# One attention stage of a fused tower: which of VectorE and GpSimd forms the products and the weighted values

## The reference

```python
x = jnp.roll(x, -W // 2, axis=1)                      # W = 64
qkv = (xw @ w_qkv.T).reshape(B * nw, W, 3, H, C // H)  # H = 8, C = 128
attn = jnp.einsum('bwhd,bwgd->bwhg', q, k) * SCALE     # 8 x 8 scores for each token
attn = jax.nn.softmax(attn, axis=-1)
out = jnp.einsum('bwhg,bwgd->bwhd', attn, v)
out = out.transpose(0, 2, 1, 3).reshape(B * nw, W, C)
out = out @ w_proj.T + b_proj                          # then rolled back, added to x
```

## Time and profile before

| | us |
|---|---|
| median of three timed runs | 1608.4 (1603.88, 1608.4, 1612.2) |
| the profiled execution | 1606.17 |
| its span, first to last instruction | 1604.5 |
| the stage in it, first matmul of q, k and v to the end of the last add | 103.3 |

### The profile page before, as it was taken

How to read it: one execution, slowest core, us unless ns; L and a number is a source line. 1 busy time by engine, 2 the same in 40 slices (tenths; PEclk the granted TensorE clock), 3 DMA queues, 4 the chain that set the end, 5 groups by cost and what they waited for, 6 DMA issues and landing times. The chain is left out here.

```text
span 1604.5 us, 29750 instructions
## 1 busy us (share of the span) xinstructions
PE 1141.8 (71%) x10322; PEld 781.8 (49%) x10330; DVE 1158.3 (72%) x2211; ACT 729.9 (45%) x1093; POOL 727.9 (45%) x626
## 2 busy tenths in 40 slices
PE   5857999984489445968777777777777785646770
PEld 3725565663389425744444444444444444435550
DVE  5666556455435447348999999999999995658983
ACT  4233443431045221025777777777767763011540
POOL 2213333231386657123555565555556553215655
PEclk9889999997589777769999999999999986858995
DMA  4052000001168300000000000000000000013772
GB/s 125 1 163 85 2 2 2 2 3 53 40 193 227 98 4 0 0 1 1 1 1 0 0 0 0 0 0 0 0 0 0 0 0 1 2 28 89 211 211 71
DMA packets 83243, 64.92 MB, mean 40 GB/s; under 512 B 13931, under 2 KB 73606, under 8 KB 82886
## 3 DMA queue, kind: packets, MB, share of 16 engines
q1 hardware_dynamic: 62726, 46.80, 10.5%
q0 software_dynamic: 4096, 8.40, 1.8%
q10 hardware_dynamic: 16320, 8.40, 1.8%
HBM read 43.64 MB, written 22.28 MB: 41 GB/s over the span
## 5 line engine op out<-in xcount | busy, mean ns | idle before, releaser
L2118 POOL TENSOR_TENSOR ta_ex<-ta_ex,ta_left 128x1024 f32<-128x1024 f32 x128 | 302.0, 2359 | 279.5 <-ACT ta_left L2061 279.5
L1962 PE MATMUL ta_ps_s<-ta_kT,ta_qz 128*128 (+1 forms) x512 | 258.6, 629 | 36.7 <-ACT ta_ex L2045 35.6
L1993 PE MATMUL ta_ps_t<-consts,ta_ex 128*128 128x128 f32 x1024 | 142.3, 283 | 111.7 <-POOL ta_ex L2118 53.0
L1993 PEld LDWEIGHTS ta_ps_t<-consts,ta_ex 128*128 128x128 f32 x1024 | 113.5, 144 | 176.0 <-POOL ta_ex L2118 137.6
L2149 DVE MAX8 ta_top<-ta_ps_s 128x8 f32<-128x1024 f32 x128 | 156.3, 1221 | 34.3 <-PE ta_ps_s L1962 33.7
L2045 ACT ACTIVATE ta_ex<-ta_ps_s,ta_ntop 128x1024 f32<-128x1024 f32 x128 | 142.7, 1115 | 49.1 <-DVE ta_left L2155 36.7
L2155 DVE MATCH_REPLACE8 ta_left<-ta_top,ta_ps_s 128x1024 f32<-128x1024 f32 x128 | 155.3, 1213 | 0.0
L2160 DVE MAX8 ta_top<-ta_left 128x8 f32<-128x1024 f32 x128 | 154.6, 1208 | 0.0
L2165 DVE MATCH_REPLACE8 ta_left<-ta_top,ta_left 128x1024 f32<-128x1024 f32 x128 | 154.6, 1208 | 0.0
L1962 PEld LDWEIGHTS ta_ps_s<-ta_kT,ta_qz 128*128 128x128 f32 x512 | 89.5, 195 | 119.1 <-issue 104.8
L2061 ACT ACTIVATE ta_left<-ta_left,ta_ntop 128x1024 f32<-128x1024 f32 x128 | 146.3, 1143 | 0.8
(11 more groups left out here) (623 smaller groups left out, 2532.4 us busy)
## 6 DMA issues: line engine op xcount, KB each, us to landing
l1e_w<-in_L_ffn_W_dram SPq DMA_DIRECT2D x46, 256.0 KB
l3e_packed<-l3f_packed SPq DMA_DIRECT2D x64, 160.0 KB, 2.9
l3f_rows<-l1f_zero SPq DMA_DIRECT2D x2, 2048.0 KB, 13.0
l3e_x<-l3f_rows SPq DMA_DIRECT2D x32, 128.0 KB, 2.9
l3e_outs<-l3e_y ACTq DMA_DIRECT2D x32, 128.0 KB, 2.7
l1f_rows<-l1f_zero SPq DMA_DIRECT2D x2, 1472.0 KB, 9.4
l1e_x<-l1f_rows SPq DMA_DIRECT2D x46, 64.0 KB
l1e_outs<-l1e_y ACTq DMA_DIRECT2D x46, 64.0 KB
```

The lines of the kernel that those rows point to most:

```text
L1962: ins = pe.matmul(ps_s[:, i % 2, half * BANK:(half + 1) * BANK], qz[:, odd, h, :], kT[:, grp, bass.ds(at.key0[i // PAIR] + half * BANK, BA ...
L1993: ins = pe.transpose(ps_t[:, j * P:(j + 1) * P], ex[:, i % 4, j * P:(j + 1) * P], m.ident)
L2118: pool.tensor_tensor(ex[:, i % 4, :], ex[:, i % 4, :], left[:, i % 4, :], ALU.subtract).then_inc(kept, 1)
```

## The change

VectorE forms the weighted values of all four tiles of a group. It also forms all four products of group 0, and those of tiles 2 and 3 of the later groups; GpSimd forms those of tiles 0 and 1 of groups 1 to 3 and nothing else. GpSimd begins group 1 when VectorE's products of group 0 are done, and group g from 2 on when the weighted values of group g - 2 are done. VectorE's list is now, for each g: scores of g (tiles 2, 3, 0, 1), products of tiles 2 and 3 of g + 1, weights of g, weighted values of g; `add(0)` stays behind the weighted values of group 2, and the scores of group 3, which were ahead of it, are behind it. The matmul and copy of q, k and v go tile by tile: 16 copies of 384 columns, each with its own signal, in place of 4 of 1536. TensorE's turning waits for VectorE alone, tile by tile. The core of the diff:

```diff
+        def operands(g, t):
+            q = qkv[:, g, t, 0:D].rearrange("p (h d) -> p h d", h=H).unsqueeze(2).broadcast_to([P, H, H, HW])
+            k = qkv[:, g, t, D:2 * D].rearrange("p (h d) -> p h d", h=H).unsqueeze(1).broadcast_to([P, H, H, HW])
+            return qk[:, slot(g, t), :, :, :], q, k
...
                 for t in range(4):
                     n = 4 * g + t
-                    ins = pe.matmul(ps_q[:, t, 0:3 * D], ...)
-                ins.then_inc(qkv_ready, 1)
+                    if g >= 1:
+                        pe.wait_ge(qkv_in, n - 3)
+                    pe.matmul(ps_q[:, t, 0:3 * D], ...).then_inc(qkv_ready, 1)
...
-                    if t < 3:
-                        pe.wait_ge(av_dve, 3 * g + t + 1)
-                    else:
-                        pe.wait_ge(av_pool, g + 1)
+                    pe.wait_ge(av_ready, 4 * g + t + 1)
...
-            for g in range(GROUPS):
-                act.wait_ge(qkv_ready, g + 1)
-                act.activation(qkv[:, g, :, :], ps_q[:, :, 0:3 * D], ACT.Copy).then_inc(qkv_in, 1)
+            for n in range(TILES):
+                act.wait_ge(qkv_ready, n + 1)
+                act.activation(qkv[:, n // 4, n % 4, :], ps_q[:, n % 4, 0:3 * D], ACT.Copy).then_inc(qkv_in, 1)
...
-            products(0)
-            for g in range(GROUPS):
-                if g + 1 < GROUPS:
-                    products(g + 1)
-                pool.wait_ge(weighed, g + 1)
-                if g >= 2:
-                    pool.wait_ge(o_turned, g - 1)
-                out, a, v = factors(g, 3)
-                pool.tensor_tensor(out, a, v, ALU.mult).then_inc(av_pool, 1)
+            for g in range(1, GROUPS):
+                pool.wait_ge(qkv_in, 4 * g + 4)
+                if g == 1:
+                    pool.wait_ge(qk_ready, 4)
+                else:
+                    pool.wait_ge(av_ready, 4 * (g - 1))
+                for t in range(2):
+                    out, q, k = operands(g, t)
+                    pool.tensor_tensor(out, q, k, ALU.mult).then_inc(qk_pool, 1)
...
+            def products(g, tiles):
+                for t in tiles:
+                    dve.wait_ge(qkv_in, 4 * g + t + 1)
+                    out, q, k = operands(g, t)
+                    dve.tensor_tensor(out, q, k, ALU.mult).then_inc(qk_ready, 1)
...
-            scores(0)
+            products(0, range(4))
             for g in range(GROUPS):
+                scores(g)
                 if g + 1 < GROUPS:
-                    scores(g + 1)
+                    products(g + 1, (2, 3))
                 weights(g)
                 dve.wait_ge(weighed, g + 1)
                 if g >= 2:
                     dve.wait_ge(o_turned, g - 1)
-                for t in range(3):
+                for t in range(4):
                     out, a, v = factors(g, t)
-                    dve.tensor_tensor(out, a, v, ALU.mult).then_inc(av_dve, 1)
+                    dve.tensor_tensor(out, a, v, ALU.mult).then_inc(av_ready, 1)
                 if g == 2:
                     add(0)
             add(B - 1)
```

More of the change, by code:

```diff
@@ L1595, in stage_l2_attn @@
             sem(x) for x in ("max_done", "shifted", "exps", "sum_done", "inverted", "weighed"))
-        av_dve, av_pool, o_turned, oT_in, spread, y_in, regrouped, yT_in, out_ready, out_used = (
-            sem(x) for x in ("av_dve", "av_pool", "o_turned", "oT_in", "spread", "y_in", "regrouped", "yT_in", "out_ready", "out_used"))
+        av_ready, qk_pool, o_turned, oT_in, spread, y_in, regrouped, yT_in, out_ready, out_used = (
+            sem(x) for x in ("av_ready", "qk_pool", "o_turned", "oT_in", "spread", "y_in", "regrouped", "yT_in", "out_ready", "out_used"))
         block = ctx.enter_context(nc.Block())
@@ L1615, in _ @@
             for g in range(GROUPS):
-                if g >= 1:
-                    pe.wait_ge(qkv_in, g)
                 for t in range(4):
                     n = 4 * g + t
-                    ins = pe.matmul(ps_q[:, t, 0:3 * D], m.xnT[:, n * P:(n + 1) * P], m.wqkv2[:, :, :].rearrange("p c d -> p (c d)"),
-                                    start=True, stop=True)
-                ins.then_inc(qkv_ready, 1)
+                    if g >= 1:
+                        pe.wait_ge(qkv_in, n - 3)
+                    pe.matmul(ps_q[:, t, 0:3 * D], m.xnT[:, n * P:(n + 1) * P], m.wqkv2[:, :, :].rearrange("p c d -> p (c d)"),
+                              start=True, stop=True).then_inc(qkv_ready, 1)
             pe.wait_ge(bias_in, 16)
@@ L1663, in exponentials @@
                 if g >= 2:
[L1664 to L1665 removed]
+                    act.wait_ge(av_ready, 4 * (g - 1))
                 act.activation(e[:, g % 2, :, :, :], s[:, g % 2, :, :, :], ACT.Exp, scale=float(HW) ** -0.5).then_inc(exps, 1)
             act.activation(prime[:, :], m.pid, ACT.Exp, scale=-1.0)
[L1669 to L1671 removed]
+            for n in range(TILES):
+                act.wait_ge(qkv_ready, n + 1)
+                act.activation(qkv[:, n // 4, n % 4, :], ps_q[:, n % 4, 0:3 * D], ACT.Copy).then_inc(qkv_in, 1)
             exponentials(0)
@@ L1699, in _ @@
         def _(pool):
-            def products(g):
-                pool.wait_ge(qkv_in, g + 1)
-                for t in range(4):
-                    if g >= 2:
[L1704 to L1707, removed]
-            products(0)
-            for g in range(GROUPS):
-                if g + 1 < GROUPS:
-                    products(g + 1)
-                pool.wait_ge(weighed, g + 1)
-                if g >= 2:
-                    pool.wait_ge(o_turned, g - 1)
-                out, a, v = factors(g, 3)
-                pool.tensor_tensor(out, a, v, ALU.mult).then_inc(av_pool, 1)
+            for g in range(1, GROUPS):
[7 more added lines that the diff above has]
+                    pool.tensor_tensor(out, q, k, ALU.mult).then_inc(qk_pool, 1)
         @block.vector
@@ L1722, in _ @@
             wide = lambda x: x[:, :].unsqueeze(2).broadcast_to([P, 4 * H, H])
-            def scores(g):
-                for t in range(4):
-                    dve.wait_ge(qk_ready, 4 * g + t + 1)
+            def products(g, tiles):
[3 more added lines that the diff above has]
+                    dve.tensor_tensor(out, q, k, ALU.mult).then_inc(qk_ready, 1)
+            def scores(g):
+                for t in (range(4) if g == 0 else (2, 3, 0, 1)):
+                    if g == 0:
+                        dve.wait_ge(qk_ready, t + 1)
+                    elif t >= 2:
+                        dve.wait_ge(qk_ready, 4 + 2 * (g - 1) + t - 1)
+                    else:
+                        dve.wait_ge(qk_pool, 2 * (g - 1) + t + 1)
                     dve.tensor_reduce(s[:, g % 2, t, :, :].rearrange("p h g -> p (h g)"),
```

## The result

The changed kernel takes 1595.0 us, the median of eight runs (1586.8 to 1598.1), beside 1612.0 us for the kernel before (eight runs, 1603.9 to 1624.8, the three of the table among them). The ratio is 0.989, 95% interval 0.986 to 0.993: faster by 17.0 us by the medians and 17.6 by the means. Forecast were 1591.5 us, 1585 to 1599, and a gain of 15.9.

What follows compares the result with a forecast made beforehand. VectorE, waiting for GpSimd's products and taking turns with it, bounds the first part, TensorE the rest. Gains of 11.5 us at the first weighting, 15.5 at the second, 15.9 after turning: 1607.4 became 1591.5 us, range 1585 to 1599.

Steps and rivals of the forecast that it cites:

- Prologue: Stage start up to the first weighting: copies by tile and products on VectorE start weighted values of group 0 11.5 us earlier.
- One cycle: From the weighting of group 0 to that of group 1: 13.6 us against 17.64, so the second weighting starts 15.5 us earlier.
- case of 1.22 us steps: VectorE steps wait for the one ahead to end, 1.22 us not 1.14: 20 steps, 1.6 us, time 1593.1; chance 0.15.
- Turn-taking: VectorE and GpSimd alternate on tensor_tensor: three weighted tiles took 7.46 us, alone about 3.5; all 16 would take 1.22 each.
- TensorE behind it: TensorE's turning of group 1: starts 1.4 us after the weighting, takes 9.6 us, ends 15.9 us earlier.
- cap that the prediction had named: ScalarE's exponential of group 2 precedes the copy of group 1's result: turning at high clock gains only 0.4 us more.
- What is late next: After group 1, TensorE's 31.3 us set the end; batch 0's add waits, group 3's first tile is ready 0.9 us early.
- Rival (d), the clock: TensorE's clock falls otherwise in projection and group 2: 1587.5 us if all full, 1597.5 if more at half; chance 0.12.

Runs made afterwards that it cites:

- The moved wait: Changed kernel, with GpSimd's products of groups 2 and 3 started beside the weighted values of groups 0 and 1, not behind them: stage 98.1 us against 86.2.
- the weighted values alone on VectorE: Kernel before, with VectorE forming all four weighted tiles and GpSimd keeping all products: stage 105.9 us against 103.3.
- The delays in groups 2 and 3: Changed kernel (stage 86.2 us) with four unused VectorE products, 4.6 us, ahead of the weights of group 2: stage 86.3 us; of group 3: 92.0 us.

## Why the prediction was right

**Prologue.** Forecast: the first weighting 16.6 us into the stage; it was 16.1. The copy took 0.49 us (0.48). The product on VectorE, the one cost without a row, took 1.22 us at steps of 1.14, as the weighted value had. The first copy was later than put, since tile 0 was done later (583.42 - 581.76 = 1.7 us in, not 1.5), and the second product began 0.14 us late for its copy. So the sums began 6.9 us into the stage, not 6.6, but the subtraction lost only 0.2 us to GpSimd, where about 1 had been put.

**One cycle.** Forecast 13.6, measured 13.54. Steps of unblocked instructions are 1.14 us for sums too: four in 4.59 is 3 x 1.13 + 1.21. The case of 1.22 us steps falls: by 4.63 us for four tensor_tensor the next one starts before the last has ended. The prediction had taken the sentence of the Trainium skill on VectorE's pipeline without its exception. The same section goes on that a next operation which isn't held starts earlier, and that is what these rows show.

**Turn-taking.** Weighted tiles at 1.22 us, sums at 1.21, no wait of a sum for GpSimd. The moved wait, and the weighted values alone on VectorE, show that the two engines' meeting is what cost the time. The Trainium skill, "SBUF — State Buffer", section "Who interferes with whom", says that the two engines share a pair of SBUF ports under an exclusive lock, that a VectorE instruction with two SBUF inputs contends for it with a GpSimd one that reads SBUF, and that a reduction never does. The 3.35 and 3.30 us beside two-input instructions, and 1.21 and 2.35 beside sums, agree.

**TensorE behind it.** Forecast 9.6 us for group 1's turning; it was 8.86, as it came to full clock after 3.2 us of it (15 instructions in that part, 51 in the 5.7 us behind), where before it took some 4.1 us. The cap that the prediction had named took hold at once: the exponential ran from 621.45, so the copy started at 621.77, 0.17 us behind the turning. Altogether TensorE was done with group 1 at 39.8 us into the stage, before 57.1, and began the regrouping 17.1 us earlier, forecast 15.9. Two terms share the 1.2 us: the second weighting came 16.1 us earlier and not 15.5, and the turning, with the cap, gave 0.6 to 0.7.

**What is late next.** 31.4 us from there to the end of group 3 (31.3). The add of batch 0 waited 5.1 us (some 6), the first tile of group 3 was ready 1.0 us before TensorE wanted it (0.9). The delays in groups 2 and 3 show both.

**Rival (d), the clock.** Inside the stage it did not fall otherwise, but for the 0.8 us in group 1's turning. It did in stages behind, in both directions from kernel to kernel, and there the prediction had looked no further than that TensorE's own instructions get longer.

**What was luck.** The mechanism of the stage was right. That the whole kernel gained the same 17 us was not sure to follow from it: without bias matmuls the stage is 28.8 us shorter than before, and by the medians the kernel gained 11.2 us in one set of runs and 14.5 in the other. In the changed kernel the stages behind happened to keep their time nearly (2.4 us more). The time itself, 1591.5 forecast and 1595.0 measured, is off by 3.5 us because the kernel before was put at 1607.4 and has a median of 1612.0 over eight runs; the larger gain took 1.1 of these 4.6 us back.

## What to carry to other kernels

When two engines share a path, ask of each pair of instructions whether it can run at once before asking which engine has too much to do: one wait, moved so that GpSimd's products meet two-input instructions again, took back 11.9 of the 17.1 us, 5.4 of them by way of TensorE's clock. A gain in a stage ends where another engine's list begins to set the end; find that list first, and look there for instructions that can go. And compare a stage by its own length in the trace: what comes behind the stage moved by up to 20 us, most of it through the clock of a later stage that was not touched.

## What the runs showed of the hardware that I had not expected

A later stage can give back more than an earlier one gains. The top-k stage took 606.5 us where the trace showed no stretch at the lower level until its last 4 us, and 629.8 at a mean clock of 0.94 in its middle. That is 23 us, 1.4% of the kernel. The Trainium skill, "TensorE: Matmul & The Clock Gate", section "Part 1: The HAM clock gate (the "warmup" mystery)", says that the number of slow matmuls varies from run to run with the gate's phase, and that the penalty of the ramp is under 1% of a typical kernel. That the number varies agrees; the phase itself was not seen here. The figure is for coming up to full clock, and the many falls of this stage cost more.

A matmul with one row between full ones costs much more than its columns. The 32 instructions of a projection with bias took 9.22 us, the 16 without it 2.05. At full clock a step is 0.21 us in the first and 0.12 in the second, so 32 steps would be 6.7 us, 4.7 more than the 16 alone take. The other 2.5 us are the fall to the lower level, which came 3.3 us into the projection although TensorE was busy all through.
